# Six local attention layers: the rotary sum and the key scaling on GpSimd, one transpose a block

## What is computed

```python
DEPTH = 6; HEADS = 16; DIM_HEAD = 64; WINDOW = 32; INNER = 1024; QK_SCALE = 8.0
def attn_layer(x, Wqkv, qs, ksc, Wo):            # x: 16 sequences x 128 tokens x 128
    q, k, v = jnp.split(x @ Wqkv, 3, -1)         # each 128 tokens x 1024, then 16 heads of 64
    ...
    q = l2norm(q) * qs
    k = l2norm(k) * ksc
    freqs, scale = rotary_tables(n)
    cos, sin = (jnp.cos(freqs), jnp.sin(freqs))
    q = q * cos * scale + rotate_half(q) * sin * scale
    k = k * cos / scale + rotate_half(k) * sin / scale
    out = local_attention(q, k, v)               # softmax over a window of 32 and the one before it
    return out.reshape(b, n, INNER) @ Wo
def ffn_layer(x, g, bln, W1, b1, W2, b2):
    ...                                          # layer norm, gated gelu, 341 wide
for i in range(DEPTH):
    x = attn_layer(shift_tokens(x), Wqkv[i], q_scale[i], k_scale[i], Wo[i]) + x
    x = ffn_layer(shift_tokens(x), ln_g[i], ln_b[i], W1[i], b1[i], W2[i], b2[i]) + x
```

## Time and profile before

| | |
|---|---|
| runs, median (lowest to highest) | 4235.33 us (4232.25 to 4241.19) |
| profiled execution, first to last instruction | 4234.2 us |
| TensorE busy | 3541.2 us, 84% of the span |
| VectorE busy | 2524.6 us, 60% |
| ScalarE busy | 2216.8 us, 52% |
| GpSimd busy | 709.7 us, 17% |
| a period of the local layers, VectorE busy | 27.2 us, 20.3 us of it |

### The profile page before, as it was taken

The page is one execution under the profiler, slowest core; times in us unless marked ns, Lnnn a source line. Parts: engine busy times, 40 slices in busy tenths (PEclk is TensorE's granted clock), DMA queues, the critical chain, the costliest instruction groups (busy, mean ns, idle before and its releaser), DMA issues.

```text
span 4234.2 us, 59682 instructions
## 1 busy us (share of the span) xinstructions
PE 3541.2 (84%) x21595; PEld 2601.5 (61%) x21707; DVE 2524.6 (60%) x4741; ACT 2216.8 (52%) x6207; POOL 709.7 (17%) x612
## 2 busy tenths in 40 slices
PE   5888888788888888888888888888888788888998
PEld 3666655566666666666666666666666655655666
DVE  2444434677777777777777777777777634444222
ACT  2433332566666665666666666666666535453332
POOL 0000000222222222222222222221222100000000
PEclk7666666999999999999999999999999967666999
DMA  5000000000000000000000000000000000000000
GB/s 140 0 0 0 0 0 0 1 0 0 0 26 0 0 0 27 0 0 0 26 0 0 0 26 0 0 0 1 1 0 0 0 0 0 0 0 0 3 2 5
DMA packets 36830, 27.61 MB, mean 7 GB/s; under 512 B 15092, under 2 KB 32526, under 8 KB 35982
## 3 DMA queue, kind: packets, MB, share of 16 engines
q1 hardware_dynamic: 36750, 26.57, 2.1%
HBM read 25.52 MB, written 1.05 MB: 6 GB/s over the span
## 4 chain that ended last, share of the span: by engine, by line
PE 70%; DVE 16%; ACT 8%; issue 3%; POOL 2%; SPq 1%; DVEq 0%; POOLq 0%; DMA 0%; ACTq 0%
PE P L461 8%; PE P L518 7%; PE P L503 5%; PE P L525 5%; PE P L343 5%; PE P L543 4%; PE P L325 3%; PE P L672 3%; PE P L657 3%; DVE bufA L899 3%; DVE bufC L901 3%; DVE bufC L942 3%; PE P L320 3%; PE P L321 2%; PE P L384 2%
## 5 line engine op out<-in xcount | busy, mean ns | idle before, releaser
L1172 POOL TENSOR_TENSOR rnorm<-sumsq_g,const_mhalf 128x16 f32<-128x16 f32 x192 | 554.5, 2905 | 1704.0 <-DVE sumsq_g L887 1704.0
L1292 ACT ACTIVATE bufA<-P,bias,rnorm 128x128 f32<-128x128 f32 x1536 | 679.0, 465 | 139.6 <-DVE bias L929 139.5
L1220 ACT ACTIVATE bufB<-P 128x512 f32<-128x512 f32 (+3 forms) x528 | 344.0, 651 | 579.5 <-PE P L483 316.0
L461 PE MATMUL P<-f_wqkv,xcT 128*128 128x512 f32 x1152 | 539.5, 604 | 73.5 <-DVE xcT L879 71.5
L518 PE MATMUL P<-bufC,vals 128*64 128x128 f32 x3072 | 312.8, 284 | 201.9 <-DVE bufC L942 201.9
L518 PEld LDWEIGHTS P<-bufC,vals 128*64 128x64 f32 x3072 | 265.2, 140 | 236.4 <-DVE bufC L942 224.9
L1220 ACT ACTIVATE vals<-P 128x1024 f32<-128x1024 f32 (+2 forms) x144 | 113.6, 789 | 542.0 <-PE P L321 332.6
L461 PEld LDWEIGHTS P<-f_wqkv,xcT 128*128 128x128 f32 x1152 | 205.1, 191 | 278.3 <-issue 259.7
L482 PE MATMUL P<-ident,bufA 128*128 128x128 f32 x1536 | 346.5, 273 | 4.1 <-DVE bufC L901 3.0
L483 PE MATMUL P<-ident,bufC 128*128 128x128 f32 x1536 | 345.8, 273 | 0.0
L1147 POOL TENSOR_TENSOR veps<-mv,const_eps 128x1 f32<-128x1 f32 x208 | 39.9, 192 | 1800.6 <-DVE mv L699 1800.6
(11 more groups left out here) (220 smaller groups left out, 6618.7 us busy)
## 6 DMA issues: line engine op xcount, KB each, us to landing
f_wqkv<-in_L_ffn_Wqkv SPq DMA_DIRECT2D x6, 1536.0 KB
f_wo<-in_L_ffn_Wo SPq DMA_DIRECT2D x6, 512.0 KB
m_w<-in_L_ffn_ew SPq DMA_DIRECT2D x1, 2048.0 KB
m_w<-in_L_ffn_ew SPq DMA_DIRECT2D x8, 256.0 KB
f_w<-in_L_ffn_W SPq DMA_DIRECT2D x6, 341.0 KB
out_x<-x_all SPq DMA_DIRECT2D x4, 256.0 KB, 2.3
f_w<-in_L_ffn_W SPq DMA_DIRECT2D x12, 64.0 KB
m_w<-in_L_ffn_sh_w SPq DMA_DIRECT2D x2, 256.0 KB
```

Source lines behind the costliest of these rows:

```text
L461: ins = pe.matmul(P[:, j, at + k * 512:at + (k + 1) * 512], xcT[:, j, 0:D], f_wqkv[:, p, lo:lo + 512], start=True, stop=True)
L1172: pool.tensor_tensor(rnorm[:, j, hs], sumsq_g[:, j, hs], const_mhalf[:], ALU.pow).then_inc(f["rn_" + s], 1)
L1220: return act.activation(dst, src, ACT.Copy, scale=scale)
L1292: ins = act.activation(bufA[:, j, k * 128:(k + 1) * 128], P[:, j, k * 128:(k + 1) * 128], ACT.Exp, bias=bias[:, j, k:k + 1], scale=rnorm[: ...
```

## The change

Two places. First, the sum of the two rotated products, which TensorE made by transposing both into one place, is made by GpSimd in `bufA` before the transpose, in one instruction of 128 x 1024 for the queries (`q_sum`) and one for the keys (`k_sum`). TensorE then transposes each block once, 16 transposes less in a period. Second, the keys are rotated as they come from the projection, without their norm, so `normalise_k` is gone; GpSimd scales the sum by the norm in two instructions of 128 x 512 (`k_scaled`). To wait for it are now `q_turned` (for `qr`) and `k_turned` (for `kr`, by half). `rotate_k` is one step instead of two and stands further ahead in VectorE's list, and `q_norms` stands last in GpSimd's.

```diff
--- before.py
+++ after.py
@@ -195,8 +195,8 @@
         core, cau = (sems(k, "scores nb probs probsT probsT_sb av rz o oT oT_sb proj") for k in ("core", "cau_core"))
         a = sems("mix", "x_in xT xT_sb kvq kvq_sb scores nb probs z rz qn oT oT_sb attn sum x1")
         x = sems("xat", "xT xT_sb qkv rope qk v qkT qkT_sb sum yn ynT ynT_sb ffn sum2 x_done")
-        f = sems("loc", "x_in xT xT_sb k q v sq_k sq_q ss_k ss_q ssg_k ssg_q rn_k rn_q t12q kn t2k v_sb qT qT_sb kT kT_sb "
-                        "negmax pn x1 tables sh xs xn xnT xnT_sb h gl g ffn x_done")
+        f = sems("loc", "x_in xT xT_sb k q v sq_k sq_q ss_k ss_q ssg_k ssg_q rn_k rn_q t12q t12k v_sb qT qT_sb kT kT_sb "
+                        "qr ksum kr negmax pn x1 tables sh xs xn xnT xnT_sb h gl g ffn x_done")
         c = sems("cau", "x_raw x_in xT xT_sb kvq kvq_sb qkT qkT_sb sum x1")
         y = sems("crs", "xT xT_sb qkv qkv_sb qkT qkT_sb sum x_done")
         m = sems("moe", "x2 x_in xT xT_sb logits router sub ex idxf share hot w wT wT_sb h g y acc x_done")
@@ -475,21 +475,14 @@
                 pe.wait_ge(f["t12q"], n + 1)
                 project_local(j, p, 0, 2, "v")
 
-            def rotated(j, lo, n):
-
-                for k in range(n):
-                    at = lo + k * 128
-                    pe.matmul(P[:, j, at:at + 128], bufA[:, j, at:at + 128], ident[:], is_transpose=True, start=True, stop=False)
-                    ins = pe.matmul(P[:, j, at:at + 128], bufC[:, j, at:at + 128], ident[:], is_transpose=True, start=False, stop=True)
-                return ins
-
             def q_turned(j, p, q, n):
                 pe.wait_ge(f["v_sb"], n + 1)
-                rotated(j, 0, 8).then_inc(f["qT"], 1)
+                pe.wait_ge(f["qr"], n + 1)
+                transposes(j, bufA[:, j, 0:INNER], 8).then_inc(f["qT"], 1)
 
             def k_turned(j, p, q, n, u):
-                pe.wait_ge(f["t2k"], n + 1)
-                rotated(j, INNER + 512 * u, 4).then_inc(f["kT"], 1)
+                pe.wait_ge(f["kr"], part(n + 1, u))
+                transposes(j, bufA[:, j, INNER + 512 * u:INNER + 512 * u + 512], 4, 8 + 4 * u).then_inc(f["kT"], 1)
 
             def score(j, p, q, n, u):
                 pe.wait_ge(f["qT_sb"], n + 1)
@@ -907,16 +900,10 @@
                 rotation(j, p, 0, 0, heads(P[:, j, 0:INNER]))
                 rotation(j, p, 0, 1, heads(P[:, j, 0:INNER])).then_inc(f["t12q"], 1)
 
-            def normalise_k(j, p, q, n):
-                dve.wait_ge(f["rn_k"], n + 1)
-                dve.tensor_tensor(heads(bufB[:, j, INNER:2 * INNER]), heads(P[:, j, INNER:2 * INNER]),
-                                  cols(rnorm[:, j, LH:], LD), ALU.mult).then_inc(f["kn"], 1)
-
-            def rotate_k(j, p, q, n, term):
-                dve.wait_ge(f["kn"], n + 1)
-                ins = rotation(j, p, 1, term, heads(bufB[:, j, INNER:2 * INNER]))
-                if term == 1:
-                    ins.then_inc(f["t2k"], 1)
+            def rotate_k(j, p, q, n):
+                dve.wait_ge(f["sq_k"], n + 1)
+                rotation(j, p, 1, 0, heads(P[:, j, INNER:2 * INNER]))
+                rotation(j, p, 1, 1, heads(P[:, j, INNER:2 * INNER])).then_inc(f["t12k"], 1)
 
             def row_maxima(j, p, q, n, u):
                 hs = slice(8 * u, 8 * u + 8)
@@ -977,8 +964,8 @@
 
             def period(b, f):
                 in_turn((x_in, f), (shift_x, f), (row_maxima, b, 1), (normalise_probs, b, 0), (rotate_q, f),
-                        (keep_turned, b, 0), (normalise_probs, b, 1), (k_squares, f), (keep_turned, b, 1), (q_squares, f),
-                        (normalise_k, f), (rotate_k, f, 0), (residual, b), (rotate_k, f, 1), (moments_local, b),
+                        (keep_turned, b, 0), (normalise_probs, b, 1), (k_squares, f), (rotate_k, f), (keep_turned, b, 1),
+                        (q_squares, f), (residual, b), (moments_local, b),
                         (normalise_local, b), (gamma_beta, b), (gated, b), (row_maxima, f, 0), (x_out, b))
 
             over_layers(dve, period, layer_tables)
@@ -1180,8 +1167,24 @@
             def inv_std_local(j, p, q, n):
                 inv_std(norm_back, BATCH + n + 1, j)
 
+            def q_sum(j, p, q, n):
+                pool.wait_ge(f["t12q"], n + 1)
+                pool.tensor_tensor(bufA[:, j, 0:INNER], bufA[:, j, 0:INNER], bufC[:, j, 0:INNER], ALU.add).then_inc(f["qr"], 1)
+
+            def k_sum(j, p, q, n):
+                pool.wait_ge(f["t12k"], n + 1)
+                both = slice(INNER, 2 * INNER)
+                pool.tensor_tensor(bufA[:, j, both], bufA[:, j, both], bufC[:, j, both], ALU.add).then_inc(f["ksum"], 1)
+
+            def k_scaled(j, p, q, n, u):
+                pool.wait_ge(f["rn_k"], n + 1)
+                pool.wait_ge(f["ksum"], n + 1)
+                half = bufA[:, j, INNER + 512 * u:INNER + 512 * u + 512].rearrange("p (h w) -> p h w", w=LD)
+                pool.tensor_tensor(half, half, cols(rnorm[:, j, LH + 8 * u:LH + 8 * u + 8], LD), ALU.mult).then_inc(f["kr"], 1)
+
             def period(b, f):
-                in_turn((k_norms, f), (q_norms, f), (inv_std_local, b))
+                in_turn((q_sum, f), (k_norms, f), (k_sum, f), (k_scaled, f, 0), (k_scaled, f, 1), (inv_std_local, b),
+                        (q_norms, f))
 
             over_layers(pool, period)
```

## The result

The changed kernel takes 4423.33 us, the median of three runs (4421.84 to 4423.42), against 4235.33: 1.0439 times the time before, with an interval of 1.0424 to 1.0453. It is slower by 188 us where 136 were forecast, and lies inside the range of 4255 to 4440. The profiled execution spans 4421.5 us.

The account below looks back on a forecast made before the run. The prediction saw no engine full and a zigzag of waits between VectorE and TensorE as the bound. It summed +1.13 - 0.87 + 1.15 = +1.41 us a period, 134 us in 95, to about 4371, range 4255 to 4440.

Parts of the forecast that it names:

- The zigzag and the slack of 1.21 us: VectorE and TensorE wait in turn; the second keep_turned was ready 1.21 us before TensorE's second weighing asked for it.
- Moved rotation, +1.13: Keys' rotation ahead of the second keep_turned on VectorE: 2.34 us, 1.21 in the slack, so +1.13 us a period.
- Transposes, -0.87, and nothing for the keys' half: TensorE works 1.75 us less; only the queries' half is on the path, -0.87 us; the keys' half lengthens idle time.
- X = 2.4: Time in us of GpSimd's sum of 1024 columns, taken as twice VectorE's, between 1.2 and 4.9.
- L925 held to the end of the sum, +1.15: VectorE's two-operand SBUF instruction before the second keep_turned waits until q_sum ends: +1.15 us a period; 52 in 100.
- the other overlaps: GpSimd's new work beside VectorE instructions with at most one operand in SBUF; no cost counted.
- nrm held by the power, 4645: Rival: q_norms' power holds the layer norm's nrm on VectorE 2.9 us on the path; within 11 in 100 above 4400.
- X above 3.0: Rival: GpSimd's sum takes over 3.0 us and its chain becomes the bound; at 3.5, 4570, or 4355 without holding.
- No disturbance, 4260: Rival: GpSimd and VectorE pass each other, X up to 3.0; +0.26 us a period, 4260; 25 in 100.
- The clock: Rival: TensorE's saving is eaten by more idle time and a lower clock grant; 3 in 100.

Follow-up runs that it names:

- e2: Changed kernel with the keys' rotation put back behind the second keep_turned on VectorE; 4277.18 us, 1.0105 times the kernel before.
- e10: Kernel before, with each keys' block turned once, from the cosine product alone (for timing only); 4238.49 us, 1.0008 times the kernel before.
- e1: Changed kernel with q_sum on GpSimd waiting until VectorE has ended the second normalise_probs (L925); 4480.64 us, 1.0597 times the kernel before.
- e4: Changed kernel with q_sum as four instructions of 128 x 256 instead of one of 128 x 1024; 4256.37 us, 1.0057 times the kernel before.
- e7: Changed kernel with the edits of both e1 and e4; 4308.04 us, 1.0169 times the kernel before.
- e8: Changed kernel with edits of e2 and e4, layer norm ahead of GpSimd's second k_scaled, norm_turned between the two k_turned; 4408.71 us.
- e9: Changed kernel with the edits of e2 and e4, and the first probs_turned done twice; 4238.59 us, 1.0005 times the kernel before.
- e3: Changed kernel with each keys' block transposed twice into the same place; 4349.09 us, 1.0275 times the kernel before.

## Why the prediction was right in the main, and where it was not

The forecast was 4371 and the time 4423, 52 us more. Put together from the runs: the schedule cost 1.15 us a step instead of 1.41, which is 25 us less than forecast; the clock cost 77 us, for which the sum had nothing. 4371 - 25 + 77 = 4423. So the range held by luck: one omission and one overestimate had opposite signs. With the schedule as forecast and the clock as it was, the time would have been 4371 + 77 = 4448, above the range.

- *The zigzag and the slack of 1.21 us.* Right. From the first weighing to the second it was 5.14 us before; now 1511.82 - 1504.65 = 7.17. That is 2.03 us more, of 2.34 + 1.15 - 1.21 = 2.28 forecast. Both announced waits are there.
- *Moved rotation, +1.13.* Right in size: from L892 to L929 2.33 us. Ahead of the second weighing the two delays add up as forecast. But moving the rotation back by itself (e2) gained 0.95 us. By the slack alone it would have been 2.34 + 0.94 - 1.21 = 2.07, since a hold of 0.94 fits into 1.21. The prediction had the hold of L925 only on VectorE's way to `keep_turned`, and TensorE also waits for it directly, 0.80 us ahead of the second `probs_turned`, while GpSimd's chain has nothing to spare in e2.
- *Transposes, -0.87, and nothing for the keys' half.* Right: 1515.95 - 1515.08 = 0.87, and e10 shows the keys' half at zero. The gap ahead of `norm_turned` went from 0.52 to 1.39 us, as said.
- *X = 2.4.* 2.35, and 1.04 for each `k_scaled`. The estimate by the GPSIMD Engine Reference of the Trainium skill, section 3.1, had been 2.25. GpSimd was in time, with 1.49 us of waiting for `mv` to spare.
- *L925 held to the end of the sum, +1.15.* The mechanism is right and settled by e1, e4, e7 and e8; the size was 0.94. From L925's start to the sum's end are 1505.89 - 1504.80 = 1.09 us, but L925 took only 0.94 longer than alone. I read this as a part of its 1.23 us that needs no data and ran meanwhile. It fits that L925 ends 1.08 us behind the sum, and L880 in e1 0.03 us behind it, each about 0.14 less than it takes alone; but no run takes that apart. This is the 0.2 us by which the term was too large. The section "Who interferes with whom" of the page SBUF — State Buffer of the Trainium skill gives this rule, and says that copies and scalings from SBUF to SBUF can be held too; L880 at 1.30, L938 at 0.89 and L696 at 1.06 us beside streaming sums agree. It doesn't agree for the power: `nrm` beside L1159 takes 0.34. The prediction priced the other overlaps at nothing, as instructions with at most one operand in SBUF. That was wrong: L880 has one and was held for 0.55 us by the keys' sum in the changed kernel. It cost nothing there, since VectorE then waited 1.72 us for TensorE anyway (L934); in e1 the guard of the keys' sums, held by `q_sum`, cost 1.13.
- *nrm held by the power, 4645.* It did not come, as the 0.34 us shows, and neither did X above 3.0. *No disturbance, 4260* was wrong as a forecast; but e4, which makes it true by other means, gave 4256.
- *The clock.* **This is the step that failed:** the sum has no term for it, and it was 77 us. I gave it 3 in 100, with the argument that the longest idle stretch, 2.11 us, had stood at a clock of 1.00, and that the new ones are shorter. They are, and 47 more steps had a fall. The row showed one period in which the clock held, not what other waits, or a step of another length, would do. e9 has falls where its longest gap is 1.32 us. A fall also costs by its place (e3), which I hadn't considered at all. In the changed kernel it came at L536, where TensorE is the bound and each us at half the clock is paid.

## What to carry over

Before work is moved to GpSimd, look at what VectorE does at that moment: here a streaming GpSimd instruction held VectorE's product of two SBUF inputs (L925) and its copies and scalings from SBUF to SBUF (L938, L880, L696) until it ended, but not its reduction (L878) or its reciprocal (L922), so cut it into pieces where such an instruction comes, rather than wait with it. When work is taken from TensorE, price the granted clock as a term of its own, with a range, and look at which work would stand under a fall. And where an improved schedule gives no time, read the clock by steps: here work that computes nothing new, in two gaps, brought 1.8%, though no rule found here says beforehand in which gaps.
